# Rotary embedding of layer 1: which engine copies, which multiplies by the cosine, which by the sine

## The reference, cut to what matters

```
def _apply_rotary(x, cos, sin):
    d2 = x.shape[-1] // 2
    x1, x2 = (x[..., :d2], x[..., d2:])
    return jnp.concatenate([x1 * cos - x2 * sin, x2 * cos + x1 * sin], axis=-1)
```

## Time and profile before

| | |
|---|---|
| median of 3 runs | 698.98 us (698.39 to 700.24) |
| profiled execution | 696.65 us, its span 695.1 us |
| PE (TensorE) busy | 650.7 us, 94% |
| DVE (VectorE) busy | 521.6 us, 75% |
| ACT (ScalarE) busy | 340.5 us, 49% |
| POOL (GpSimd) busy | 319.7 us, 46% |
| granted TensorE clock | 1.00 throughout |

### The profile page before, as it was taken

One profiled execution on the slowest core, in us unless ns is written; L12 is line 12 of the kernel. 1 busy time (PEld: TensorE's weight loads), 2 busy tenths in 40 slices (PEclk: granted clock), 3 DMA queues, 4 the chain that ended last, 5 costly groups with the idle time before them and its releaser, 6 DMA issues.

```text
span 695.1 us, 13353 instructions
## 1 busy us (share of the span) xinstructions
PE 650.7 (94%) x4780; PEld 491.5 (71%) x4780; DVE 521.6 (75%) x1068; ACT 340.5 (49%) x740; POOL 319.7 (46%) x255
## 2 busy tenths in 40 slices
PE   3999999999899999999999999998999999899987
PEld 1455555578568787988878797887977845757766
DVE  4287867674679979799797998657436897789994
ACT  1476111120356565555756555575435573379441
POOL 1000788600176747486674747889619632120000
PEclk9999999999999999999999999999999999999999
DMA  8801000000420101010010101111422200000001
GB/s 249 338 1 63 1 1 1 2 0 1 143 108 9 40 15 38 23 38 23 8 38 15 38 23 39 36 36 33 149 68 55 70 0 0 15 25 0 1 1 60
DMA packets 14645, 31.34 MB, mean 45 GB/s; under 512 B 1837, under 2 KB 8587, under 8 KB 14029
## 3 DMA queue, kind: packets, MB, share of 16 engines
q1 hardware_dynamic: 12813, 26.46, 11.6%
q0 software_dynamic: 1536, 3.15, 1.7%
q10 hardware_dynamic: 256, 1.18, 0.6%
HBM read 26.59 MB, written 5.24 MB: 46 GB/s over the span
## 4 chain that ended last, share of the span: by engine, by line
PE 44%; DVE 22%; issue 11%; ACT 10%; POOL 9%; DMA 3%; DVEq 1%; SPq 0%; POOLq 0%; ACTq 0%
PE bank L569 8%; PE bank L578 7%; PE bank L588 5%; PE bank L589 4%; PE bank L590 4%; DVE x L1700 3%; PE bank L805 2%; DVE arena L1675 2%; DVE arena L1674 2%; DVE arena L1684 2%; PE bank L804 2%; PE bank L775 2%; DMA arena<-in_lA 2%; PE bank L789 2%; POOL arena L2104 2%
## 5 line engine op out<-in xcount | busy, mean ns | idle before, releaser
L588 PE MATMUL bank<-zone 128*128 128x256 f32 (+1 forms) x408 | 139.6, 342 | 13.8 <-DVE arena L1675 6.0
L589 PE MATMUL bank<-zone 128*128 128x256 f32 (+1 forms) x408 | 131.1, 321 | 0.0
L590 PE MATMUL bank<-zone 128*128 128x256 f32 (+1 forms) x408 | 131.1, 321 | 0.0
L2118 POOL TENSOR_TENSOR arena<-arena 128x512 f32<-128x512 f32 x64 | 82.1, 1283 | 62.2 <-ACT arena L1268 62.1
L588 PEld LDWEIGHTS bank<-zone 128*128 128x128 f32 x408 | 76.9, 189 | 34.7 <-DVE arena L1675 10.7
L2123 POOL TENSOR_TENSOR arena<-arena 128x512 f32<-128x512 f32 x64 | 83.2, 1299 | 26.9 <-DVE arena L1675 18.0
L590 PEld LDWEIGHTS bank<-zone 128*128 128x128 f32 x408 | 76.9, 189 | 6.1
L569 PE MATMUL bank<-xT,arena 128*128 128x512 f32 x160 | 78.0, 627 | 2.1 <-DMA arena<-in_lA 0.8
L589 PEld LDWEIGHTS bank<-zone 128*128 128x128 f32 x408 | 77.1, 189 | 3.4
L1287 ACT ACTIVATE arena<-arena 128x256 f32<-128x256 f32 (+1 forms) x128 | 62.1, 487 | 33.7 <-DVE arena L1684 33.1
L1700 DVE SCALAR_TENSOR_TENSOR x<-bank,arena,x 128x256 f32<-128x256 f32 x128 | 52.9, 470 | 13.7 <-PE bank L590 13.5
(11 more groups left out here) (292 smaller groups left out, 1344.0 us busy)
## 6 DMA issues: line engine op xcount, KB each, us to landing
arena<-in_qk SPq DMA_DIRECT2D x16, 256.0 KB, 2.6
arena<-in_tern SPq DMA_DIRECT2D x1, 3072.0 KB, 22.4
arena<-in_wv SPq DMA_DIRECT2D x8, 256.0 KB, 2.9
arena<-in_wo SPq DMA_DIRECT2D x16, 128.0 KB, 2.1
arena<-in_wr SPq DMA_DIRECT2D x1, 1792.0 KB, 9.7
lB<-in_lB SPq DMA_DIRECT2D x1, 1288.5 KB, 24.9
x<-in_x SPq DMA_DIRECT2D x2, 512.0 KB, 8.0
xg_rows<-arena SPq DMA_DIRECT2D x1, 1024.0 KB
```

The source lines that it names most:

```text
L588: pe.matmul(dst, lhi, rhi, start=(n == 0), stop=False)
L589: pe.matmul(dst, lhi, rlo, start=False, stop=False)
L590: last = pe.matmul(dst, llo, rhi, start=False, stop=(n == len(terms) - 1 and not open_end))
L2118: pool.tensor_tensor(qraw[:, j, :], qraw[:, j, :], cosT[:, at], ALU.mult).then_inc(cos_done, 1)
```

## The change

ScalarE copies the two halves of a bank in two instructions, each to the opposite half of a tile `qturn` (the old `qraw`). VectorE multiplies the bank by the cosine in one instruction on 128 partitions. GpSimd multiplies `qturn` by the sine and adds. The host table changes the order of its two sine halves, since they are now read by the destination's partition.

```
-                act.activation(qraw[:, j, :], ps[j % 2], ACT.Copy).then_inc(raw_kept, 1)
+                act.activation(qturn[0:64, j, :], ps[j % 2][64:128, :], ACT.Copy)
+                act.activation(qturn[64:128, j, :], ps[j % 2][0:64, :], ACT.Copy).then_inc(raw_kept, 1)
...
-                dve.tensor_tensor(qsin[0:64, j, :], ps[j % 2][64:128, :], sinT[64:128, at], ALU.mult)
-                dve.tensor_tensor(qsin[64:128, j, :], ps[j % 2][0:64, :], sinT[0:64, at], ALU.mult).then_inc(rope_half, 1)
+                dve.tensor_tensor(qcos[:, j, :], ps[j % 2], cosT[:, at], ALU.mult).then_inc(rope_half, 1)
...
-                    pool.tensor_tensor(qraw[:, j, :], qraw[:, j, :], cosT[:, at], ALU.mult).then_inc(cos_done, 1)
-                    pool.wait_ge(cos_done, h * 4 + (j + 1))
+                    pool.tensor_tensor(qturn[:, j, :], qturn[:, j, :], sinT[:, at], ALU.mult).then_inc(sin_done, 1)
+                    pool.wait_ge(sin_done, h * 4 + (j + 1))
...
-                    pool.tensor_tensor((kT1, qT1)[j % 2][:, at], qraw[:, j, :], qsin[:, j, :], ALU.add).then_inc(qk_ready, 1)
+                    pool.tensor_tensor((kT1, qT1)[j % 2][:, at], qturn[:, j, :], qcos[:, j, :], ALU.add).then_inc(qk_ready, 1)
...
-    cossin = np.concatenate([np.tile(np.cos(freq), (2, 1)), np.concatenate([np.sin(freq), -np.sin(freq)], 0)], 1).astype(f32)
+    cossin = np.concatenate([np.tile(np.cos(freq), (2, 1)), np.concatenate([-np.sin(freq), np.sin(freq)], 0)], 1).astype(f32)
```

More of the change, by code:

```diff
@@ L229, in build @@
         affT_ready = sem("affT_ready")
-        xT1_kept, cos_done = sem("xT1_kept"), sem("cos_done")
+        xT1_kept, sin_done = sem("xT1_kept"), sem("sin_done")
         xT_hi, wqk_hi, wqk_split, wo_hi, wo_split, raw_kept, oT1_hi = (
@@ L298, in build @@
         qT1, kT1, v1 = m.cols(T), m.cols(T), m.grid(NT, 2 * DH)
-        qsin = m.grid(4, BW)
+        qcos = m.grid(4, BW)
         S1_at = m.at
@@ L319, in build @@
         assert y.at <= m.at
-        qraw = m.grid(4, BW)
+        qturn = m.grid(4, BW)
         xg = xT.rearrange("p k t -> p (k t)").rearrange("p (t d) -> p t d", t=NT)
```

## The result

The changed kernel takes 717.91 us (714.64 to 719.26, 4 runs) against 699.5 us (4 runs): ratio 1.0265, 95% interval 1.024 to 1.0289. It is 18 us slower, where 3 were forecast. The direction was right, the time lies far outside the range of 695.5 to 706.

What follows compares the result with a forecast made beforehand. ScalarE's full queue, with TensorE waiting on it, was taken as the bound. Terms 0 + 1.8 + 0.6 + 0.55 = 2.95, say 3.0 us, added to the 698.98 median gave 702.0; range 695.5 to 706.0.

Steps and rivals of the forecast that it cites:

- ScalarE in the even head has no time in hand: Even head, last product with the values: ScalarE's last copy ends 0.81 us later, so TensorE starts at 344.26 instead of 343.45.
- The price c of the second copy: ScalarE's queue, each of four pieces a head: one more copy, on 64 partitions, costs 0.48 us, at most 0.60.
- A pair gets longer by 7c - 2.92: Even plus odd head: seven added copies less ScalarE's slack of 1.11, 0.41 and 1.40; 0.44 us at c = 0.48.
- heads 2 to 9: Four pairs of heads in layer 1, each longer by 0.45 us: 1.8 us in the sum.
- The start and head 0: Start of layer 1 and heads 0, 1: VectorE's gain and ScalarE's idle time leave 0, give or take 0.4 us.
- the two pairs behind: Heads 10 and 11 add 0.6 us through ScalarE's queue; heads 12 and 13 add 0.55, mostly through GpSimd's.
- The rule on ScalarE's overlap: ScalarE copies: 186 ns plus 0.833 ns per element, neighbours overlapping by 93 ns; c 0.52, sum 4.5 us, time 703.5.
- VectorE gains 0.69 on each piece: VectorE's rotary multiplies: one on 128 partitions replaces two on 64, saving 0.69 us a piece, 2.8 a head.
- Rival A: VectorE's relief decides if c is under 0.42: 693 us at best, 695.5 to 696.5 if half is kept; chance 0.20.
- Rival B: Same ScalarE price, but VectorE absorbs the lateness by the odd head's maxima: pair 0.1 us longer, 700.2; chance 0.22.
- Rival C: GpSimd becomes the bound, each piece reaching it 0.48 us later: price 6.7 us, time 705.7; chance 0.08.
- The range: Whole time: 695.5 us, taking in half of A, up to 706.0, for c = 0.60 and C.

Runs made afterwards that it cites:

- two full copies: The changed kernel, but both ScalarE copies take all 128 partitions and the exchange of halves is left out; ratio 1.0018 to the kernel before.
- straight halves: The changed kernel, but ScalarE's two copies of 64 partitions go straight, without the exchange of halves; ratio 1.0247 to the kernel before.
- kernel after: The changed kernel itself, with ScalarE's two crossing copies of 64 partitions in all four pieces, against the kernel before; 717.91 us, ratio 1.0265.
- the quarters above: The kernel before, ScalarE's copy cut into four (64 partitions, 256 columns each) in pieces 0 and 1, into 96 and 32 partitions in pieces 2 and 3; 719.0 us.
- piece 0 alone: The kernel before, with the change made only for piece 0 of heads 1 to 15, ScalarE exchanging the halves and GpSimd subtracting; ratio 0.9955.

## Why the prediction was wrong, step by step

- **ScalarE in the even head has no time in hand, and TensorE will wait before the last product.** Right: place, waiter and releaser are those of the rows.
- **The price c of the second copy, 0.48, bounded above by 0.60.** This is the step that failed. Half the partitions indeed save nothing, but c is not one start-to-start step. It is what the queue lengthens by between a full instruction ahead and one behind: 0.62 + 0.605 + 0.61 where there had been 0.48 + 0.48, so 0.88. The prediction took the step from full copies (335.11 to 335.58) and assumed that it holds for halves; the upper bound, a copy standing alone, left out that the copy's neighbours lose their overlap too. The hint stood in the trace of before: VectorE's two multiplies of 64 partitions started 0.705 apart, longer than their 0.693, while its full ones overlapped.
- **A pair gets longer by 7c - 2.92.** Right. That it holds to 0.1 us is luck in part: it takes the slack of both heads as it stood at a c of half the size, and has no term for the second wait. With c as each kernel's steps give it:

```
kernel                 steps (us)             c      pair by formula   measured
two full copies        0.48 0.48 0.48         0.48   41.20             41.23
straight halves        0.49 0.59 0.62         0.74   43.3              43.24
kernel after           0.62 0.605 0.61        0.88   44.0              43.93
```

For straight halves the two pieces 1 of the pair count with 0.86 each (0.21 + 0.605 + 0.62 against 0.09 + 0.48); with 0.74 throughout the formula gives 43.0. With 0.88 in the sum, heads 2 to 9 give 4 x 3.2 = 13 us (measured 12.5 in heads 1 to 8) instead of 1.8. The start and head 0 came to 1.2 together, the two pairs behind to 2.7 and 4.0 (1.7 of it the clock's); the prediction had 0, 0.6 and 0.55. Those were not worked out again one by one.
- **The rule on ScalarE's overlap** gave c = 0.52 by the same assumption. The Trainium skill, "ScalarE: Activation LUTs", section "What ACT_TABLE_LOAD costs", has neighbours overlap by about 93 ns and names no condition; 0.1 us is what the full copies show, and nothing is what the halves of the changed kernel show.
- **VectorE gains 0.69 on each piece.** Nearly right in busy time (46.4 us over 64 pieces, 0.73 each). In its queue it is 0.8, since a full multiply gets its overlap back: L1675 to the next instruction is 0.61, where two narrow ones took 1.42.
- **Rival A** (the relief decides if c is under 0.42): its best case was 693 from 698.98, 6 us; with no second copy at all it came to 9. The changed kernel was far on the other side of its condition. **Rival B** (the forecast's price for ScalarE, a pair 0.1 longer): it shared the wrong price; at the c of 0.48 that it assumed, the two full copies lengthened a pair by 0.47, not by 0.1. **Rival C** (GpSimd): no TensorE wait behind it in the even heads; at the start of head 13 TensorE's wait for it went down from 2.11 to 0.3 us, as TensorE came late.
- **The range** went up to 706.0 on c = 0.60. The sum was steep in c (7 times per pair), so its bound had to be sought at another form of instruction, and the bound chosen was no bound.

## What to carry to other kernels

Price an instruction put into a full queue by the starts around it: how far apart were its neighbours, and how far will they be. On ScalarE, splitting a copy by partitions cost 0.74 to 0.88 us and doubling it 0.48, since each change of the first partition takes away the overlap on its border. Splitting by columns should cost least: two pieces of 256 columns at 0.28 against one step of 0.48 make 0.1 us, an estimate from the quarters above. If an engine's queue has slack at some pieces only, make the change there: piece 0 alone turned 18 us of loss into 3 of gain.

## What the runs showed of the hardware

Two ScalarE copies from PSUM with 512 columns in float32 took about 0.6 each and started 0.48 to 0.49 apart when both began on partition 0, the second on 128, 96 or 64 partitions behind a full one; 0.58 to 0.62 apart when the second began on partition 64 or 96 or returned from there to 0; 0.61 to 0.62 when an instruction wrote to another half than it read. With 256 columns: 0.28 against 0.377. The last ScalarE instruction that used the same memory counts, not the neighbour alone: 0.21 instead of 0.09 behind an accumulator read on partition 0, where the last read of PSUM had begun on 64. On VectorE the steps were 0.705 between the two crossing halves of 64 partitions and 0.61 behind a full multiply, at 0.69 each; straight halves were not run there. GpSimd's multiply took 1.28 us on 64 partitions, crossing, as on 128 (where it exchanges piece 0 and in the kernel before).
